# Three gates' state passes in a row, the key-value product behind them, the next tile's keys ahead of the context

## The chip, the cores and the metric

The kernel runs on one core of one Trainium2 chip. The metric is the device time of one execution in microseconds (us); lower is better. The whole input and output stay in fp32.

## What is computed

Eight tiles (`T = 8`) of 512 rows of 128 features. A linear attention, a layer norm, a gated recurrence over the eight tiles, and a second layer norm:

```
Q = elu(x @ Wq.T + bq) + 1;  K = elu(x @ Wk.T + bk) + 1;  V = x @ Wv.T + bv
KV = einsum('bnd,bne->bde', K, V);  Z = einsum('bnd,bd->bn', Q, K.sum(axis=1) + 1e-06)
x  = layernorm(x + (einsum('bnd,bde->bne', Q, KV) / Z[..., None]) @ Wo.T + bo)
# recurrence over the leading axis t = 0..7, state c per row and feature
ft = sigmoid(xt @ wf.T + c @ uf.T + bf);  it = sigmoid(xt @ wi.T + c @ ui.T + bi)
gt = tanh(xt @ wc.T + c @ uc.T + bc);     c  = ft * c + it * gt
h  = tanh(x @ wo.T + c_final @ uo.T + bo);  out = layernorm(x + h)
```

## The kernel before

Every engine has a queue written out by hand, and semaphores tie the queues together. A tile goes through stages that are spread over several tiles in flight. The loop `periods()` runs six times; in period `a` the keys and queries of tile `k = a + 1`, the key-value product and context of tile `a`, the residual and layer norm of tile `b = a - 1`, and the recurrence step of tile `t = a - 2` are worked on. Behind the loop an outro, written call by call, finishes tiles 6 and 7 and steps 4 to 11 (from step 4 on a step handles half a tile, 256 columns), then comes the output projection with the second layer norm.

What each stage does, and its line in the rows:

- `keys` (PE, L430): eight matmuls into the one bank `ps_k`. `key_exp` (ACT, L771), `key_max` (DVE, L1048) turn them into `k_rows`; `key_bias` (ACT, L841) then puts the bias into `ps_k` for the next `keys`. `keys(n)` waits for all three of the tile before.
- `queries` (PE, L448 to L454), `query_exp` (ACT), `query_sum` (DVE, L1106). `x_high` and `x_low` (DVE, L1100) split the next tile's columns into two parts.
- `keys_x` (PE, L463), copied by `xk_copy` (ACT, L855); `key_sums` on POOL (L330, L335). From both `key_values` on PE (L473, L474) makes the key-value product, and `key_values` on DVE (L1114) writes it to `kvo`.
- `context` (PE, L483) waits for `kvo`. `reciprocal_z` (DVE, L1027), `residual` (L1036), `statistics` (L1006), `variance` (L1012), the root on POOL (L339) and `normalise` (DVE, L1021) make the first layer norm.
- `x1_turned` (PE, L497) transposes the normed tile into the one bank `ps_x1`; `x1_high` (ACT, L859) and `x1_low` (DVE, L1043) split it; `x1_whole` (ACT, L863) copies it and frees the bank.
- `gates_x` (PE, L517, L519, L526): nine passes, six that need the high part of the tile and then three that need the low part. `gate_s` (PE, L544, L546, L549): three passes of one gate with the old state, `gates_s` all three gates. Then the three tanh (ACT, L785), `kept_state` (DVE, L1059), `new_state` (L1066), `next_state` (L1073), `state_high` (ACT, L801), `state_low` (POOL, L371).

The order of PE in periods 3 to 5 before is: `keys(k)`, a transpose in period 3, `queries(k)`, `gates_x(t)`, `keys_x(a)`, the forget gate's state passes, `key_values(a)`, the other two gates' state passes, `context(a)`, `x1_turned(b)`. The order of DVE from `attention_end(b)` on is: residual, statistics, variance, `key_max(k)`, `query_sum(k)`, `x_low(k + 1)`, `key_values(a)`, `normalise(b)`, `kept_state(t)`, `new_state(t)`, `reciprocal_z(a)`, `next_state(t)`, `x1_low(b)`.

Of the kernel before, what the change touches and what calls it, by code (L numbers as in the profile page):

```python
# [86 lines left out]
def build(nc, x, xt, w_kq, w_vo_in, w_gate, w_out, rows, att_row, out):  # L87
    with ExitStack() as ctx:
# [323 lines left out]
        def _(pe):  # L412
# [118 lines left out]
            def gates_x(k):  # L531
                for g in range(GATES):
                    gate_x_high(g, k)
                for g in range(GATES):
                    gate_x_low(g, k)
# [131 lines left out]
            for k, a, b, t in periods():  # L667
                if a == 0:

                    keys_x(a)  # L670
                    keys(k)
                    key_values(a)
                    queries(k)
                    context(a)
                    continue

                keys(k)
                if a == 1:
                    keys_x(a)
                if a in (2, 3):  # L680
                    x1_turned(a - 2)
                queries(k)
                if t == 0:

                    gate_x_high(0, t)
                    keys_x(a)
                    gate_x_low(0, t)
                    gate_x_high(1, t)
                    key_values(a)
                    gate_x_low(1, t)  # L690
                    gate_x_high(2, t)
                    gate_x_low(2, t)
                    context(a)
                    continue
                if t is not None:
                    gates_x(t)
                    keys_x(a)
                    gate_s(0, t)
                key_values(a)
                if a == 1:  # L700
                    setup_gates()
                if t is not None:
                    gate_s(1, t)
                    gate_s(2, t)
                context(a)
                if b >= 2:
                    x1_turned(b)

            keys(7)
            queries(7)  # L710
            gates_x(4)
            keys_x(6)
            gate_s(0, 4)
            key_values(6)
            keys_x(7)
            gate_s(1, 4)
            gate_s(2, 4)
            context(6)
            key_values(7)
            x1_turned(5)  # L720
            context(7)
            gates_x(5)
            gates_s(5)
            gates_x(6)
            gates_s(6)
            x1_turned(6)
            out_x(0)
# [33 lines left out]
        def _(act):  # L761
# [112 lines left out]
            for k, a, b, t in periods():  # L874
                if a == 0:
                    xk_copy(a)
                key_exp(k)
                if a == 1:
                    xk_copy(a)
                    act.wait_ge(halved_ok, 1)  # L880
                    nc.scalar.activation(wgate_hi[:, GATES:2 * GATES], wgate[:, GATES:2 * GATES],
                                         ACT.Copy).then_inc(split_hi, 1)
                if t is not None and t >= 1:
                    state_high(t - 1)
                if t is not None:
                    x1_whole(t)
                if a == 2:
                    xk_copy(a)
                query_exp(k)
                if b == 0:  # L890
                    first_normalise(b)
                if a == 0:

                    act.wait_ge(gate_in, 16)
                    nc.scalar.activation(wgate_hi[:, 0:GATES], wgate[:, 0:GATES], ACT.Copy).then_inc(split_hi, 1)
                if k + 1 >= FIRST_SPLIT:
                    x_high(k + 1)
                if a > 2:
                    xk_copy(a)
                if t is not None:  # L900
                    forget_tanh(t)
                    key_bias(k + 1)
                    input_tanh(t)
                if b is not None:
                    x1_high(b)

            key_exp(7)
            state_high(3)
            x1_whole(4)
            query_exp(7)  # L910
            xk_copy(6)
            forget_tanh(4)
            xk_copy(7)
# [44 lines left out]
        def _(dve):  # L958
# [128 lines left out]
            def attention_end(b):  # L1087

                residual(b, range(H, C), y_small_ok)
                residual(b, range(H), y_ok)  # L1090
                dve.wait_ge(y_ok, b + 1)
                dve.wait_ge(y_small_ok, b + 1)
                statistics(b)
                variance(b)
# [28 lines left out]
            for k, a, b, t in periods():  # L1123
# [23 lines left out]
                    query_sum(k)  # L1147
                if k + 1 >= FIRST_SPLIT:
                    x_low(k + 1)
                if a > 2:  # L1150
                    key_values(a)
                normalise(b)
                if a == 1:
                    split_low()
                    first_biases()
                    query_sum(k)
                if t is not None:
                    kept_state(t)
                    new_state(t)
                    reciprocal_z(a)  # L1160
                    next_state(t)
                if b >= 1:
                    x1_low(b)

            attention_end(5)
            key_max(7)
            query_sum(7)
            key_values(6)
            normalise(5)
            kept_state(4)  # L1170
            new_state(4)
            reciprocal_z(6)
            key_values(7)
            next_state(4)
            residual(6, range(H, C), y_small_ok)
            x1_low(5)
            residual(6, range(H), y_ok)
# [129 lines left out]
```

## Time and profile before

| | |
|---|---|
| three runs | 100.78, 101.58 and 101.7 us, median 101.58 us |
| the profiled execution | 101.45 us, of which the span from first to last instruction is 99.7 us |
| PE, DVE, ACT, POOL busy | 90.2, 83.8, 68.8 and 39.9 us |
| granted TensorE clock, mean | 0.975; it is down only in the last two of 40 slices |

PE is TensorE's matmuls, DVE is VectorE, ACT is ScalarE, POOL is GpSimd. The 1.75 us between the execution's time and its span lie ahead of the first and behind the last instruction. In the rows below, matmuls overlap: the next one starts before the one ahead of it has ended, so what a group takes is read from start to start.

### The profile page before, as it was taken

Reading aid. Unit: us, or ns where it says so; the run is one execution under the profiler, and the core shown is the slowest. Engines: PE = TensorE matmul, PEld = TensorE weight load, DVE = VectorE, ACT = ScalarE, POOL = GpSimd, SP = SyncE. Lnnn points to the kernel's source line nnn. Section 1 sums busy time; section 2 is a strip of 40 time slices with the busy share of each in tenths; the row PEclk is TensorE's granted clock in tenths of the full one; section 3 lists DMA queues with packets and bytes.
Section 4 is the critical chain, followed back from the end, with each engine's and each line's share of the span. In section 5 each row is a group of like instructions: output and inputs, shape, how many; then the busy total and the mean of one; then the engine's idle time right before and its main releaser. Section 6 shows DMA issues by size and latency. Waiting matters only on the chain.

```text
span 99.7 us, 1926 instructions
## 1 busy us (share of the span) xinstructions
PE 90.2 (91%) x610; PEld 79.0 (79%) x610; DVE 83.8 (84%) x240; ACT 68.8 (69%) x143; POOL 39.9 (40%) x55
## 2 busy tenths in 40 slices
PE   5998999999999999999999999999999999999000
PEld 4677798778687888898899899999999999896000
DVE  3058489997999999999999989999857897999970
ACT  1428479479698588869778546759586678899460
POOL 3006198508447317606903812440110324445750
PEclk9999999999999999999999999999999999999955
DMA  1868999100000000000000000000000002032636
GB/s 33 290 227 316 396 398 360 54 0 3 0 0 0 0 7 0 3 0 0 0 0 0 0 7 0 0 7 0 7 0 0 0 0 101 5 112 92 224 105 211
DMA packets 5413, 7.36 MB, mean 74 GB/s; under 512 B 507, under 2 KB 3228, under 8 KB 5404
## 3 DMA queue, kind: packets, MB, share of 16 engines
q1 hardware_dynamic: 4972, 6.92, 19.3%
q10 hardware_dynamic: 432, 0.33, 1.3%
q8 instruction: 5, 0.08, 0.3%
q14 instruction: 4, 0.03, 0.1%
HBM read 5.15 MB, written 2.10 MB: 73 GB/s over the span
## 4 chain that ended last, share of the span: by engine, by line
PE 72%; DVE 14%; ACT 6%; issue 2%; POOL 1%; DVEq 0%; ACTq 0%
PE ps_k L430 8%; PE ps_ctx L483 7%; PE ps_ctx L463 6%; DVE stats L1218 4%; PE ps_x L497 4%; PE ps_f L417 4%; DVE x L1237 4%; PE ps_q L454 3%; DVE x L1207 2%; PE ps_ctx L473 2%; PE ps_f L517 2%; PE ps_ctx L474 2%; PE ps_f L526 1%; ACT k_exp L771 1%; PE ps_c L517 1%
## 5 line engine op out<-in xcount | busy, mean ns | idle before, releaser
L371 POOL TENSOR_TENSOR s_lo<-s,s_hi 128x512 fp32r<-128x512 f32 (+1 forms) x6 | 6.7, 1110 | 23.1 <-ACT s_hi L801 23.1
L339 POOL TENSOR_TENSOR rstd<-var_eps,minus_half 128x4 f32<-128x4 f32 x8 | 8.7, 1090 | 8.1 <-DVE var_eps L1012 7.9
L364 POOL TENSOR_TENSOR rstd<-var_eps,minus_half 128x4 f32<-128x4 f32 (+1 forms) x9 | 8.8, 983 | 3.5 <-DVE var_eps L1225 3.3
L330 POOL TENSOR_TENSOR k_pair<-k_rows 128x256 f32<-128x256 f32 x8 | 6.2, 780 | 9.5 <-DVE k_rows L1048 9.5
L859 ACT ACTIVATE x_hi<-ps_x 128x512 fp32r<-128x512 f32 x8 | 4.8, 603 | 6.6 <-PE ps_x L497 6.6
L1021 DVE TENSOR_SCALAR x<-x,stats,rstd 128x128 f32<-128x128 f32 x28 | 9.3, 390 | 0.0
L430 PE MATMUL ps_k<-wkq,x_cols 128*128 128x128 f32 x64 | 9.2, 290 | 0.0
L771 ACT ACTIVATE k_exp<-ps_k,minus_one 128x512 f32<-128x512 f32 x8 | 5.5, 687 | 5.3 <-PE ps_k L438 4.4
L430 PEld LDWEIGHTS ps_k<-wkq,x_cols 128*128 128x128 f32 x64 | 8.4, 204 | 0.7 <-DMA wkq<-w_kq 0.6
L1036 DVE SCALAR_TENSOR_TENSOR x<-ps_ctx,z_inv,x_rows 128x128 f32<-128x128 f32 x28 | 8.0, 342 | 0.1
L483 PEld LDWEIGHTS ps_ctx<-kvo,q_cols 128*128 128x128 f32 x56 | 7.1, 191 | 1.1 <-issue 0.9
L463 PEld LDWEIGHTS ps_ctx<-k_rows,x_rows 128*128 128x128 f32 x56 | 7.1, 191 | 1.0 <-issue 0.7
L463 PE MATMUL ps_ctx<-k_rows,x_rows 128*128 128x128 f32 x56 | 7.5, 277 | 0.4 <-DVE k_rows L1048 0.4
L483 PE MATMUL ps_ctx<-kvo,q_cols 128*128 128x129 f32 x56 | 7.5, 277 | 0.0
L1066 DVE SCALAR_TENSOR_TENSOR new<-th_i,th_c 128x256 f32<-128x256 f32 (+1 forms) x12 | 6.1, 509 | 1.5 <-ACT th_c L785 1.4
L1073 DVE SCALAR_TENSOR_TENSOR s<-keep,new 128x256 f32<-128x256 f32 (+1 forms) x12 | 6.2, 513 | 0.8
L1006 DVE BATCH_NORM_STATS2 stats<-x 128x6 f32<-128x256 f32 x16 | 6.2, 426 | 0.2
L827 ACT ACTIVATE x<-x,shift,rstd 128x128 f32<-128x128 f32 x13 | 5.6, 485 | 1.0 <-DVE shift L1231 0.8
L1048 DVE SCALAR_TENSOR_TENSOR k_rows<-k_exp,ps_k 128x512 f32<-128x512 f32 x8 | 5.4, 681 | 1.0 <-ACT k_exp L771 1.0
L776 ACT ACTIVATE q_exp<-ps_q,wkq 128x512 f32<-128x512 f32 x8 | 5.5, 687 | 0.9 <-PE ps_q L454 0.8
L1059 DVE SCALAR_TENSOR_TENSOR keep<-th_f,s 128x256 f32<-128x256 f32 (+1 forms) x11 | 5.4, 490 | 0.8 <-ACT th_f L785 0.8
L801 ACT ACTIVATE s_hi<-s 128x256 fp32r<-128x256 f32 (+1 forms) x10 | 4.9, 497 | 1.7 <-DVE s L1073 1.6
(219 smaller groups left out, 292.1 us busy)
## 6 DMA issues: line engine op xcount, KB each, us to landing
x_cols<-xt SPq DMA_DIRECT2D x8, 256.0 KB, 7.0
x_rows<-x SPq DMA_DIRECT2D x8, 256.0 KB, 7.0
out<-x SPq DMA_DIRECT2D x7, 256.0 KB, 2.2
wgate<-w_gate SPq DMA_DIRECT2D x1, 384.0 KB, 6.5
out<-x SPq DMA_DIRECT2D x2, 128.0 KB, 2.0
wkq<-w_kq ACTq DMA_DIRECT2D x1, 131.0 KB, 4.0
wvo_in<-w_vo_in ACTq DMA_DIRECT2D x1, 128.0 KB, 4.0
wout<-w_out SPq DMA_DIRECT2D x1, 128.0 KB, 6.7
```

The costliest lines, as they stand in the source:

```text
L330: nc.gpsimd.tensor_tensor(k_pair[:], k_rows[:, a % 2, 0:C // 2], k_rows[:, a % 2, C // 2:C], ALU.add).then_inc(k_pair_ok, 1)
L339: nc.gpsimd.tensor_tensor(rstd[:, b], var_eps[:, b], minus_half[:], ALU.pow).then_inc(rstd_ok, 1)
L364: nc.gpsimd.tensor_tensor(part_of(rstd, u, T), part_of(var_eps, u, T), minus_half[:, 0:nt * H].rearrange("p (t c) -> p t c", c=H), ALU.pow ...
L371: nc.gpsimd.tensor_tensor(s_lo[:, t % 2, part], state(t)[:, part], s_hi[:, t % 2, part].bitcast(F32), ALU.subtract).then_inc(slo_ok[k], 1)
L430: mm = nc.tensor.matmul(ps_k[:, c * D:(c + 1) * D], x_cols[:, a, c], wkq[:, WK_T * D:(WK_T + 1) * D], start=(c == 0 and a < BIAS_BY_PE), s ...
L463: mm = nc.tensor.matmul(small(a)[:, 0:D], x_rows[:, a, c], k_rows[:, a % 2, c], start=(c == 0), stop=(c == C - 1))
L483: mm = nc.tensor.matmul(ctx_of(b, c // 2)[:, c % 2], q_cols[:, b % 2, c], kvo[:, b % 2], start=True, stop=True, skip_group_check=True)
L771: nc.scalar.activation(k_exp[:, a % 2].rearrange("p c d -> p (c d)"), ps_k[:], ACT.Exp, bias=minus_one[:, 0:1]).then_inc(k_exp_ok, 1)
L1006: st = nc.vector.bn_stats(stats[:, b, c:c + 2].rearrange("p c m -> p (c m)"), x1[:, b, c:c + 2].rearrange("p c d -> p d c"))
L1021: nc.vector.tensor_scalar(x1[:, b, c], x1[:, b, c], mean_of(b, c), rstd[:, b, c:c + 1], ALU.subtract, ALU.mult).then_inc(x1_ok, 1)
L1036: ins = nc.vector.scalar_tensor_tensor(x1[:, b, c], ctx_of(b, c // 2)[:, c % 2, 0:D], z_inv[:, b % 2, c:c + 1], x_rows[:, b, c, 0:D], ALU. ...
L1073: nc.vector.scalar_tensor_tensor(state(t)[:, part], keep[:, part], 0.5, new[:, part], ALU.mult, ALU.add).then_inc(s_ok, 1)
```

## The change

On PE, `keys(k)` leaves the head of periods 4 and 5 and of the outro; `keys(k + 1)` is put between `key_values(a)` and `context(a)` of periods 3 to 5. The three gates' state passes of steps 1 to 4 stand in a row ahead of `key_values(a)`. In step 6 the third gate's first passes are put last. On ACT, `key_exp` follows `keys` to the end of the period, ahead of `x1_high`, and `x1_whole` goes behind `query_exp` in periods 4 and 5 and in the outro. On DVE, `key_values(a)` moves from ahead of `normalise(b)` to behind `kept_state(t)`, `next_state(t)` ahead of `reciprocal_z(a)`, and `x1_low` of tiles 2 to 4 into the following `attention_end`, behind the residual. No instruction is added or taken away.

```diff
@@ PE
-                keys(k)
+                if a <= 3:
+                    keys(k)
...
                 if t is not None:
                     gates_x(t)
                     keys_x(a)
-                    gate_s(0, t)
+                    gates_s(t)
                 key_values(a)
...
                 if t is not None:
-                    gate_s(1, t)
-                    gate_s(2, t)
+                    keys(k + 1)
                 context(a)
...
-            keys(7)
             queries(7)
             gates_x(4)
             keys_x(6)
-            gate_s(0, 4)
+            gates_s(4)
             key_values(6)
             keys_x(7)
-            gate_s(1, 4)
-            gate_s(2, 4)
             context(6)
...
             gates_s(5)
-            gates_x(6)
+            for g in (0, 1):
+                gate_x_high(g, 6)
+            for g in (0, 1):
+                gate_x_low(g, 6)
+            gate_x_high(2, 6)
+            gate_x_low(2, 6)
             gates_s(6)
@@ ACT
-                key_exp(k)
+                if a <= 3:
+                    key_exp(k)
...
-                if t is not None:
+                if a in (2, 3):
                     x1_whole(t)
                 if a == 2:
                     xk_copy(a)
                 query_exp(k)
+                if a > 3:
+                    x1_whole(t)
...
                     forget_tanh(t)
                     key_bias(k + 1)
                     input_tanh(t)
+                if t is not None and t >= 1:
+                    key_exp(k + 1)
                 if b is not None:
                     x1_high(b)
 
-            key_exp(7)
             state_high(3)
+            query_exp(7)
             x1_whole(4)
-            query_exp(7)
@@ DVE, attention_end(b)
                 residual(b, range(H, C), y_small_ok)
                 residual(b, range(H), y_ok)
+                if b >= 3:
+                    x1_low(b - 1)
@@ DVE, the loop
-                if a > 2:
-                    key_values(a)
                 normalise(b)
...
-                if t is not None:
+                if t == 0:
                     kept_state(t)
                     new_state(t)
                     reciprocal_z(a)
                     next_state(t)
-                if b >= 1:
+                if t is not None and t >= 1:
+                    kept_state(t)
+                    key_values(a)
+                    new_state(t)
+                    next_state(t)
+                    reciprocal_z(a)
+                if b == 1:
                     x1_low(b)
...
-            key_values(6)
             normalise(5)
             kept_state(4)
+            key_values(6)
             new_state(4)
+            next_state(4)
             reciprocal_z(6)
             key_values(7)
-            next_state(4)
             residual(6, range(H, C), y_small_ok)
```

## Rows read from the trace of the kernel before

**Rows 1.** The page's fourth part: the chain that ended last, by engine.
```profile
PE 72%; DVE 14%; ACT 6%; issue 2%; POOL 1%; DVEq 0%; ACTq 0%
```

**Rows 2.** Busy time of each engine in two stretches, one period of PE each.
```profile
core 0: us, PE busy (x) PEld busy (x) DVE busy (x) ACT busy (x) POOL busy (x), PEclk, DMA share, GB/s
34.80:43.25 8.45, 8.45 (x56) 7.44 (x55) 8.37 (x21) 6.77 (x12) 3.81 (x4) 1.00 0.01 3
43.25:51.69 8.44, 8.44 (x55) 7.44 (x55) 8.36 (x21) 6.76 (x12) 3.82 (x4) 1.00 0.00 0
```

**Rows 3.** Timeline of PE, a period in full flow: start, us, instruction, output and inputs.
```profile
41.76 1.05 PE L483 MATMUL ps_ctx<-kvo,q_cols 128*128 128x129 f32 x8
42.65 0.60 PE L497 MATMUL ps_x<-ident,x 128*128 128x128 f32 x4
43.09 1.06 PE L430 MATMUL ps_k<-wkq,x_cols 128*128 128x128 f32 x8
43.90 0.48 PE L448 MATMUL ps_q<-x_hi,wq_hi 128*128 128x512 f32 x1
...
44.68 0.39 PE L517 MATMUL ps_f<-x_hi,wgate_hi 128*128 128x512 f32 x1
...
46.77 1.05 PE L463 MATMUL ps_ctx<-k_rows,x_rows 128*128 128x128 f32 x8
...
48.36 0.39 PE L473 MATMUL ps_ctx<-bias_z,k_sum 128*128 128x129 f32 x2
```

**Rows 4.** Timeline of PE in period 3, the first with state passes.
```profile
30.29 0.48 PE L544 MATMUL ps_f<-s_hi,wgate_hi 128*128 128x512 f32 x1
...
33.24 1.13 PE L483 MATMUL ps_ctx<-kvo,q_cols 128*128 128x129 f32 x8
...
35.45 0.47 PE L448 MATMUL ps_q<-x_hi,wq_hi 128*128 128x512 f32 x1
```

**Rows 5.** Timeline of DVE in period 3.
```profile
31.68 1.25 DVE L1100 TENSOR_TENSOR x_lo<-x_cols,x_hi 128x512 fp32r<-128x512 f32 x1
32.86 0.28 DVE L1114 TENSOR_TENSOR kvo<-ps_ctx,eps_z 128x129 f32<-128x129 f32 x1
33.06 1.10 DVE L1021 TENSOR_SCALAR x<-x,stats,rstd 128x128 f32<-128x128 f32 x4
34.08 0.68 DVE L1059 SCALAR_TENSOR_TENSOR keep<-th_f,s 128x512 f32<-128x512 f32 x1
```

**Rows 6.** Timeline of ACT, the transposed tile's high part; in brackets idle time and releaser.
```profile
43.29 0.60 ACT L859 ACTIVATE x_hi<-ps_x 128x512 fp32r<-128x512 f32 x1 [0.64 <-PE ps_x L497]
```

**Rows 7.** Timeline of DVE at the end of period 5 and in the outro.
```profile
52.59 0.68 DVE L1043 TENSOR_TENSOR x_lo<-ps_x,x_hi 128x512 fp32r<-128x512 f32 x1
53.19 1.12 DVE L1036 SCALAR_TENSOR_TENSOR x<-ps_ctx,z_inv,x_rows 128x128 f32<-128x128 f32 x4
...
55.82 0.68 DVE L1106 SCALAR_TENSOR_TENSOR q_cols<-q_exp,q_relu 128x512 f32<-128x512 f32 x1
...
56.71 1.53 DVE L1021 TENSOR_SCALAR x<-x,stats,rstd 128x128 f32<-128x128 f32 x4
58.16 0.41 DVE L1059 SCALAR_TENSOR_TENSOR keep<-th_f,s 128x256 f32<-128x256 f32 x1
```

**Rows 8.** Timeline of POOL in the outro.
```profile
55.39 1.02 POOL L339 TENSOR_TENSOR rstd<-var_eps,minus_half 128x4 f32<-128x4 f32 x1 [0.21 <-DVE var_eps L1012]
56.38 0.72 POOL L330 TENSOR_TENSOR k_pair<-k_rows 128x256 f32<-128x256 f32 x1
```

**Rows 9.** Timeline of PE in the outro.
```profile
53.11 0.28 PE L517 MATMUL ps_f<-x_hi,wgate_hi 128*128 128x256 f32 x1
...
54.18 1.06 PE L463 MATMUL ps_ctx<-k_rows,x_rows 128*128 128x128 f32 x8
...
55.78 0.46 PE L473 MATMUL ps_ctx<-bias_z,k_sum 128*128 128x129 f32 x2 [0.16 <-ACT xk L855]
...
57.92 1.05 PE L483 MATMUL ps_ctx<-kvo,q_cols 128*128 128x129 f32 x8
```

**Rows 10.** The list of waits: who waited for whom, us in total, times, longest.
```profile
PEld ps_k L517 <- DVE x L1036: 0.2, 1, 0.2
```

## The prediction, made before the changed kernel was run

> **What bounds the kernel now.** I read the page's chain first: 72% of it lies on PE, 14% on DVE, and none of the waits in it is long [rows 1]. Then the busy time by stretches: in the two full periods PE is busy for all of 8.45 and 8.44 us, and DVE for 8.37 and 8.36 [rows 2]. So in the steady part PE has no gap that a new order could close, DVE is only just behind it, and the same work in another order can't make a period shorter. Gaps that could be closed are the few in period 3 and the outro: 0.16 us at `key_values(6)` [rows 9] and 0.2 us at step 6's third gate, which waits for the residual of tile 7 [rows 10]. On the other side every gap that the new order opens is paid in full, since from period 3 to the outro's end PE never gets ahead of its work.
>
> What PE needs, from start to start: the context's eight matmuls 42.65 - 41.76 = 0.89, the transposes 0.44, keys 0.81, queries 0.78, nine gate passes 46.77 - 44.68 = 2.09, so 0.23 each [rows 3]. From `key_values` at 48.36 to the next context at 50.20 (41.76 and 8.44) lie six passes, 1.40, which leaves 0.44 for the product. Keys ahead of the context are taken at the context's 0.89.
>
> **Period 3, `kvo(3)`.** Before, `key_values(3)` on DVE runs at 32.86, ahead of the normalise, and the context starts at 33.24, 0.10 after its end [rows 4, 5]. Up to there DVE's queue is as before and without a gap, so its next instruction still starts at 32.86. Now come the normalise (34.08 - 33.06 = 1.02) and `kept_state` (0.68, less the 0.08 by which neighbours overlap) ahead of it: `kvo(3)` starts at 34.49, ends at 34.77, and the context can start at 34.87. PE is there earlier: state passes from 30.29 [rows 4], nine of them 2.18 (the first one after an fp32 group takes 0.32), product 0.44, `keys(5)` 0.89, so at 33.80. It waits 1.07 us. Context and refill take 0.96 as before (35.45 less keys, less transposes, less 33.24), transposes without keys behind them 0.36, so `queries(5)` start at 36.19 against 35.45 [rows 4]: **+0.74**. What was gained is in this sum: no wait for the product's inputs, and the keys are already done. The moved keys add a wait of their own, for `key_bias`, which stands behind the forget gate's tanh in ACT's queue: two instructions of 0.6 to 0.7 us like that of rows 6, while PE has six passes and the product, 1.84, to do; nothing is lost. They hide 0.89 of the DVE work; without them the wait would be 1.96. Behind the waiting context nothing on PE can pass, and DVE's `reciprocal_z` waits for it.
>
> **Three times the transposed tile.** `x1_high` on ACT starts 43.29 - 42.65 = 0.64 after the transposes' start and ends at 1.24 [rows 3, 6]. The gates' first pass needs it. Before, keys and queries lay between: 44.68 - 42.65 = 2.03 [rows 3]. With the keys gone it is 2.03 - 0.89 = 1.14, less than 1.24 and the 0.10 of a signal. PE waits 0.20 and needs 0.07 to refill (0.96 against 0.89 at the context): 0.27 in periods 4 and 5 and in the outro, together **+0.8**. Bounds: nothing, if the first pass starts early by the overlap that the timeline draws, and 0.4 each, if `key_exp`, now ahead of `x1_high` in ACT's queue, is late; `keys` end one context (0.89) before the transposes start, and its 0.69 fits into that, so I take 0.27. `state_high` on ACT and `state_low` on POOL now follow `x1_high`; they are needed only behind `gates_x` and `keys_x`, 2.9 us of PE's work later [rows 3].
>
> **`x1_low` behind the residual.** It costs 0.60 wherever it stands [rows 7]. After the context's end come reciprocal 0.17, residual 1.15, `x1_low` 0.68, so it ends some 2.2 after the transposes' start. The low passes of a full step come after six high ones, at about 2.8: nothing in periods 4 and 5. In the outro the six are half as wide, (54.18 - 53.11) / 9 = 0.12 each [rows 9], and come at 2.1: 0.2 lost, but the next point takes its place.
>
> **DVE's chain to `kvo(6)`.** `queries(7)` now start at 52.34 (8.44 after 43.90, rows 3) + 0.74 + 2 x 0.27 = 53.62, the transposes at S = 53.26. From S: the context's end and reciprocal to 0.38, residual to `query_sum` 55.82 - 53.19 = 2.63 and `x1_low` 0.60, to 3.61; `query_sum` 0.60, to 4.2; the root of 1.02 ends about there too [rows 8]; normalise 58.16 - 56.71 = 1.45 [rows 7], `kept_state` 0.34, `kvo` 0.29 and the signal: 6.48. So `context(6)` starts at 59.74 against 57.92 [rows 9]. PE itself, with two `keys_x`, `gates_x`, the state passes and the product, would be there at S + 6.0, so it waits about 0.5. The shift is now 1.8. Step 6's new order gives back the 0.2 of its wait and a refill [rows 10]: **+1.6** when PE goes on. From there to the last 20 us nothing changes in the order, PE is full, and the tail on DVE starts from a gate of PE; the shift is carried to the end. `next_state` ahead of the reciprocal puts 0.6 between `kvo` and it, while the context takes 0.89: nothing. Of the other moves, `x1_whole` behind `query_exp` costs nothing: it only has to be done before the next transposes, seven microseconds later.
>
> **A rule weighed.** The normalise of tile 5 takes 1.53 for the same four instructions that take 1.10 in period 3, and POOL's `k_pair` runs at 56.38 to 57.10 beside it [rows 5, 7, 8]; `x_low` takes 1.25 where other 512-wide DVE instructions take 0.68 [rows 5, 7]. That DVE and POOL hold each other up explains both. If the normalise of tile 5 were not held up, `context(6)` would be 0.43 earlier and the sum +1.2. The Trainium skill, "SBUF — State Buffer", section "Who interferes with whom", says that an instruction of DVE with two SBUF inputs, or in a two-port mode, and a GpSimd instruction that reads SBUF exclude each other for their whole length; by that rule, with which these rows agree, the hold-up stays.
>
> **Sum.** The execution of 101.45, + 0.74 + 0.54 + 0.5 (third stall and chain) - 0.2 = 103.05, so 103.1. The runs' median lies 0.13 higher than the profiled execution, which I leave out.
>
> **The rivals.** *Faster: the order closes the gaps and opens none.* The product behind nine passes no longer waits for `xk`: in the outro it starts at 55.78, where `keys_x` at 54.18 with 0.81 and three half passes with 0.44 would allow 55.43, so 0.35 [rows 9]; step 6 no longer waits, 0.2 [rows 10]; and in period 3 the context starts at 33.24 where passes from 30.29 and the product would allow 32.91, so 0.33 [rows 4]. Together 0.9, so 100.55. The point from which it decides: DVE must have `kvo(3)` written by 33.7, but it stands behind a queue without a gap until 34.77. For it speaks only that modelled ends and POOL's spans are rough. Chance 0.09.
> *Swallowed.* Only period 3's +0.74 stays, the transposes' high part comes in time, and what is saved at the outro's product and at step 6 (0.35 and 0.2) sets off the rest: 101.4 to 102.5, likeliest 102. For it: the 0.20 wait rests on a difference of two tenths. Against it: the chain to `kvo(6)` has two tenths less to spare than it needs even so. Chance 0.24.
> *DVE becomes the bound of every period.* Its work is 8.4 of 8.4 [rows 2]. From the context's end to the next `kvo` now lie residual, `x1_low`, statistics, keys, queries, `x_low`, normalise and `kept_state`, some 7.0, and the context itself is 0.89 to 1.1: 8.1 to 8.2, below PE's 8.7 with its waits. Were each normalise held up as that of tile 5, 0.43 more, it would be 8.6; still no more than PE. With another half microsecond per period 104. Chance 0.07.
>
> **How the numbers follow.** My forecast has 0.60. Its own range: without the refills and with a free normalise + 0.8 less 0.25, 102.0; with 0.4 at each transpose and nothing back at step 6, 103.9. Less than 1% is no more than a measurement of this kernel can tell from no change, here 100.6 to 102.6 around the median. The forecast's lower end falls into that with 0.05. Faster by over 1% has 0.09 less what is too small, 0.07; within 1% 0.24 + 0.05 + 0.02 = 0.31; slower 0.62. The range of 8 in 10 takes in the upper half of the swallowed case: 101.6 to 103.9.
>
> **What would show it.** Right: in period 3 an idle PE of about 1 us ahead of the context, released by DVE's L1114; in periods 4 and 5 a first gate pass that waits for ACT's `x_hi`; 8.7 us per period; `context(6)` released by `kvo`; no wait at step 6's third gate. Wrong: DVE running ahead of PE in period 3, a period of 8.44 still, or a tail on DVE that starts no later than now.

## The result, and the profile after

The changed kernel takes 103.81 us (median of 6 runs, 103.16 to 104.03) against 101.47 us (6 runs, 100.74 to 101.83) on the same chip: a ratio of 1.0236, 95% interval 1.0201 to 1.0272. Its profiled execution took 103.16 us, its span is 101.4 us; 101.45 and 99.7 us before.

The chain that ended last, by engine, has moved from PE to DVE and to waiting ("issue") [rows 1]:

```profile
PE 69%; DVE 17%; issue 5%; ACT 5%; POOL 1%; DVEq 0%; ACTq 0%
```

Busy time of each engine in the two full periods, from one `queries` to the next, with the columns of [rows 2]:

```profile
35.57:44.35 8.78, 8.70 (x56) 7.43 (x55) 8.29 (x20) 6.61 (x12) 3.81 (x4) 1.00 0.01 3
44.35:53.13 8.78, 8.70 (x56) 7.44 (x55) 8.39 (x21) 6.61 (x12) 3.81 (x4) 1.00 0.00 0
```

A period is 8.78 us against 8.44 before. The work is the same; what was added is a wait.

PE in period 3 and at the head of period 4 (to be read against [rows 4] and [rows 3]):

```profile
32.16 1.06 PE L430 MATMUL ps_k<-wkq,x_cols 128*128 128x128 f32 x8
34.25 1.13 PE L483 MATMUL ps_ctx<-kvo,q_cols 128*128 128x129 f32 x8 [1.03 <-issue]
35.22 0.60 PE L497 MATMUL ps_x<-ident,x 128*128 128x128 f32 x4
35.57 0.47 PE L448 MATMUL ps_q<-x_hi,wq_hi 128*128 128x512 f32 x1
...
36.60 0.47 PE L517 MATMUL ps_f<-x_hi,wgate_hi 128*128 128x512 f32 x1
```

DVE in period 3, against [rows 5]:

```profile
30.92 1.26 DVE L1108 TENSOR_TENSOR x_lo<-x_cols,x_hi 128x512 fp32r<-128x512 f32 x1
32.10 1.24 DVE L1027 TENSOR_SCALAR x<-x,stats,rstd 128x128 f32<-128x128 f32 x4
33.27 0.67 DVE L1065 SCALAR_TENSOR_TENSOR keep<-th_f,s 128x512 f32<-128x512 f32 x1
33.87 0.27 DVE L1122 TENSOR_TENSOR kvo<-ps_ctx,eps_z 128x129 f32<-128x129 f32 x1
```

ACT at two of the three transposes, against [rows 6]:

```profile
35.85 0.60 ACT L861 ACTIVATE x_hi<-ps_x 128x512 fp32r<-128x512 f32 x1 [1.91 <-PE ps_x L497]
...
44.63 0.60 ACT L861 ACTIVATE x_hi<-ps_x 128x512 fp32r<-128x512 f32 x1 [0.64 <-PE ps_x L497]
```

Both waits that were foretold stand in these rows. `kvo(3)` ends at 34.14 and the context starts at 34.25, though `keys(5)` from 32.16 take 0.89 and PE was there at 33.05: 1.20 from start to start. The page puts the wait down to "issue", without a name; that it is `kvo` follows from DVE's row, which ends 0.11 before. And the first gate pass, at 36.60, starts 0.15 after `x_hi` ends at 36.45; the three query passes before it need 0.78 and would have let it start at 36.35.

The outro: DVE against [rows 7], POOL against [rows 8], PE against [rows 9].

```profile
51.81 0.69 DVE L1072 SCALAR_TENSOR_TENSOR new<-th_i,th_c 128x512 f32<-128x512 f32 x1 [0.22 <-ACT th_c L787]
...
54.47 0.68 DVE L1049 TENSOR_TENSOR x_lo<-ps_x,x_hi 128x512 fp32r<-128x512 f32 x1
...
57.17 1.80 DVE L1027 TENSOR_SCALAR x<-x,stats,rstd 128x128 f32<-128x128 f32 x4
58.89 0.41 DVE L1065 SCALAR_TENSOR_TENSOR keep<-th_f,s 128x256 f32<-128x256 f32 x1
59.22 0.28 DVE L1122 TENSOR_TENSOR kvo<-ps_ctx,eps_z 128x129 f32<-128x129 f32 x1
```

```profile
57.11 0.73 POOL L330 TENSOR_TENSOR k_pair<-k_rows 128x256 f32<-128x256 f32 x1
```

```profile
54.16 0.36 PE L517 MATMUL ps_f<-x_hi,wgate_hi 128*128 128x256 f32 x1
...
55.21 0.38 PE L526 MATMUL ps_f<-x_lo,wgate_hi 128*128 128x256 f32 x1
...
57.62 0.38 PE L473 MATMUL ps_ctx<-bias_z,k_sum 128*128 128x129 f32 x2
...
59.61 1.13 PE L483 MATMUL ps_ctx<-kvo,q_cols 128*128 128x129 f32 x8 [0.49 <-issue]
...
65.48 0.32 PE L517 MATMUL ps_k<-x_hi,wgate_hi 128*128 128x256 f32 x1
```

`context(6)` is released by `kvo` (59.50), the product no longer waits for `xk`, and step 6's third gate starts without a wait.

**How the kernels are compared below.** The head of the span varies from execution to execution: before, the first weights of `keys(0)` wait 0.64 us for the load of `wkq`, and in the changed kernel's profile they don't. The transposes of period 3, `x1_turned(1)`, start at 25.64 before, at 24.88 after, and between 24.81 and 26.16 in the other kernels, none of which is altered ahead of them. So I count from that instruction. Before, `context(6)` starts 57.92 - 25.64 = 32.28 later and the span ends 74.06 later; after, 34.73 and 76.52. The change costs **2.45 us by `context(6)` and 2.46 at the end**. The medians say 2.34. Each ratio is to the kernel before on the same chip, whose median was 101.24 beside e1 to e4, 101.30 beside e5 to e8 and 101.45 beside e9 to e12. Most rows rest on 4 runs, e11 on 10, e6, e7 and e12 on 12; a fourth run of e4, in a slow state at 181.44 us, is left out. Line numbers of DVE and ACT differ by a few from kernel to kernel; the names of the tiles don't.

| kernel | median us | ratio to before, 95% interval | `x1_turned(1)` | `context(6)` | span | shift at `context(6)` | at the end |
|---|---|---|---|---|---|---|---|
| after | 103.81 | 1.024, 1.020 to 1.027 | 24.88 | 59.61 | 101.4 | +2.45 | +2.46 |
| e1_kvo3_early | 103.23 | 1.020, 1.014 to 1.026 | 25.65 | 60.20 | 102.0 | +2.27 | +2.29 |
| e2_keys_back | 106.61 | 1.053, 1.047 to 1.060 | 25.20 | 62.30 | 104.1 | +4.82 | +4.84 |
| e8_keys_back_high_first | 104.75 | 1.038, 1.031 to 1.045 | 25.16 | 60.80 | 102.5 | +3.36 | +3.28 |
| e3_turned_first | 102.79 | 1.014, 1.009 to 1.019 | 24.93 | 59.23 | 101.0 | +2.02 | +2.01 |
| e4_pool_later | 102.80 | 1.014, 1.006 to 1.021 | 25.88 | 59.22 | 101.4 | +1.06 | +1.46 |
| e5_turned_pool | 102.59 | 1.014, 1.008 to 1.019 | 25.57 | 58.94 | 101.1 | +1.09 | +1.47 |
| e9_row_only | 103.21 | 1.016, 1.011 to 1.022 | 24.86 | 58.56 | 100.5 | +1.42 | +1.58 |
| e10_low_later | 102.83 | 1.015, 1.010 to 1.019 | 24.92 | 59.29 | 101.0 | +2.09 | +2.02 |
| e11_keys_only | 102.20 | 1.009, 1.006 to 1.012 | 26.16 | 59.35 | 101.1 | +0.91 | +0.88 |
| e6_before_pool | 101.21 | 0.998, 0.995 to 1.001 | 24.81 | 56.95 | 98.7 | -0.14 | -0.17 |
| e7_before_step6 | 101.27 | 1.000, 0.996 to 1.003 | 25.36 | 57.63 | 99.3 | -0.01 | -0.12 |
| e12_before_pool_step6 | 100.89 | 0.996, 0.993 to 1.000 | 25.35 | 57.42 | 99.1 | -0.21 | -0.31 |

### The profile page after: what moved, and what is told of

Read it like the earlier page. It is cut to its first block, busy times and chain, and to the rows that moved or that the text cites. A ratio compares the mean times of both kernels' runs of the same rounds, so it can differ in the third digit from the quotient of the medians.

```text
span 101.4 us, 1926 instructions
## 1 busy us (share of the span) xinstructions
PE 90.2 (89%) x610; PEld 79.0 (78%) x610; DVE 84.7 (84%) x240; ACT 68.2 (67%) x143; POOL 39.8 (39%) x55
## 4 chain that ended last, share of the span: by engine, by line
PE 69%; DVE 17%; issue 5%; ACT 5%; POOL 1%; DVEq 0%; ACTq 0%
PE ps_ctx L463 7%; PE ps_k L430 6%; PE ps_ctx L483 6%; DVE stats L1230 4%; PE ps_f L417 4%; DVE x L1249 4%; PE ps_q L454 3%; PE ps_x L497 3%; DVE x L1219 2%; PE ps_f L517 2%; PE ps_f L526 2%; DVE new L1072 2%; DVE s L1079 2%; ACT th_i L787 1%; PE ps_i L526 1%
## 5 line engine op out<-in xcount | busy, mean ns | idle before, releaser
L1027 DVE TENSOR_SCALAR x<-x,stats,rstd 128x128 f32<-128x128 f32 x28 | 10.1, 416 | 0.0
L430 PE MATMUL ps_k<-wkq,x_cols 128*128 128x128 f32 x64 | 8.6, 277 | 0.0
```

Of the source, the lines that this page charges most:

```text
L430: mm = nc.tensor.matmul(ps_k[:, c * D:(c + 1) * D], x_cols[:, a, c], wkq[:, WK_T * D:(WK_T + 1) * D], start=(c == 0 and a < BIAS_BY_PE), s ...
L1027: nc.vector.tensor_scalar(x1[:, b, c], x1[:, b, c], mean_of(b, c), rstd[:, b, c:c + 1], ALU.subtract, ALU.mult).then_inc(x1_ok, 1)
```

## Experiments on the changed kernel

**e1_kvo3_early: is it `kvo(3)` behind `kept_state` that costs period 3?** In period 3 alone `kvo` goes back ahead of the normalise.

```diff
+                if a == 3:
+                    key_values(a)
                 normalise(b)
...
                     kept_state(t)
-                    key_values(a)
+                    if a > 3:
+                        key_values(a)
```

> The changed kernel, but DVE writes kvo(3) ahead of the normalise of tile 2, as before the change; kvo(4) to kvo(6) stay behind kept_state. Theory A (DVE's queue is the bound wherever a new wait shows): PE's 1.03 us ahead of context(3) go, but normalise, kept_state, new_state, next_state and the reciprocal are as late as they were, so x1_low(2) ends at about the same time and PE waits some 0.6 us ahead of the low gate passes of period 4; of 1.1 us only about 0.5 come back: 103.3 us. Rival B (the wait at context(3) is a cost of its own, placed by the order of two instructions): all of 1.0 to 1.1 us comes back, 102.7 us.

The wait at `context(3)` is gone, but the end moves by 0.17 us only. The timeline of PE has the reason:

```profile
33.83 1.06 PE L483 MATMUL ps_ctx<-kvo,q_cols 128*128 128x129 f32 x8
...
38.36 0.50 PE L526 MATMUL ps_f<-x_lo,wgate_hi 128*128 128x512 f32 x1 [0.62 <-DVE x_lo L1049]
```

`queries(5)` come 0.38 earlier than before the change (9.43 against 9.81 after `x1_turned(1)`), then the low passes stop PE for 0.62. DVE's rows name a single wait there, 0.17 ahead of `kvo`, and its `x_lo` is ready no earlier than in the changed kernel (12.65 against 12.51 after `x1_turned(1)`), so PE meets DVE at the next tile that it needs. The 103.3 of the one theory is met, not the 102.7 of the other. The wait for `kvo(3)` is not a cost of its own: it is one of the places where PE is brought back to DVE's pace.

**e3_turned_first: do the transposes ahead of the context take the `x_hi` wait away?**

```diff
                     keys(k + 1)
-                context(a)
                 if b >= 1:
                     x1_turned(b)
+                context(a)
```

> The changed kernel, but in periods 3 to 5 the transposes of tile b stand ahead of the context of tile a. They fill 0.44 us of the wait ahead of context(3), and x_hi is ready when the gates ask for it. Theory A: PE then waits for DVE instead: ahead of the low passes of steps 2 and 4 and still ahead of context(6), and only 0.2 to 0.3 us come back, 103.5 us. Rival C: 0.44 + 3 x 0.33 = 1.4 us come back, 102.4 us.

Periods are 8.69 and 8.66 (`queries` at 35.20, 43.89, 52.55) in place of 8.78, and the first gate passes wait for nothing. But half of the wait for `kvo(3)` remains, and the low passes of the outro now wait:

```profile
34.31 1.13 PE L483 MATMUL ps_ctx<-kvo,q_cols 128*128 128x129 f32 x8 [0.52 <-issue]
...
54.83 0.38 PE L526 MATMUL ps_f<-x_lo,wgate_hi 128*128 128x256 f32 x1 [0.62 <-DVE x_lo L1049]
```

The end gains 0.45 us, and the time lies between the two that were expected. A period is still 0.22 to 0.25 longer than before the change; what takes it is seen in e5.

**e4_pool_later: what does POOL's work beside DVE cost?** POOL's `key_sums(a)`, from tile 4 on, waits until the normalise of tile `a - 2` is done, so the two no longer overlap.

```diff
             def key_sums(a):
+                if a >= 4:
+                    pool.wait_ge(x1_ok, x1_done(a - 2, C - 1))
```

> The changed kernel, but POOL's key sums of tiles 4 to 7 wait until DVE has written the whole normalise of two tiles before, so that they no longer run beside x_low and normalise. If DVE and POOL hold each other up: x_low takes 0.7 instead of 1.24 us, the normalise 1.1 instead of 1.24, and 1.1 instead of 1.8 in the outro; PE's wait ahead of context(3) falls from 1.03 to about 0.2, that ahead of context(6) goes, 1.3 us come back: 102.5 us, all of it by an engine that is not the bound of a period. If the long instructions are long by themselves: durations and time stay, 103.8 us, or a little more by the added wait.

DVE, POOL and PE in the timeline of this kernel:

```profile
31.93 0.68 DVE L1110 TENSOR_TENSOR x_lo<-x_cols,x_hi 128x512 fp32r<-128x512 f32 x1
...
34.36 1.01 DVE L1074 SCALAR_TENSOR_TENSOR new<-th_i,th_c 128x512 f32<-128x512 f32 x1
...
57.44 1.12 DVE L1029 TENSOR_SCALAR x<-x,stats,rstd 128x128 f32<-128x128 f32 x4
...
58.68 0.79 POOL L332 TENSOR_TENSOR k_pair<-k_rows 128x256 f32<-128x256 f32 x1 [1.28 <-PE ps_ctx L476]
...
61.90 0.68 PE L485 MATMUL ps_k<-kvo,q_cols 128*128 128x129 f32 x4 [0.70 <-DVE kvo L1124]
```

`x_low` falls from 1.26 to 0.68, the normalise of the outro from 1.80 to 1.12, `context(6)` waits for nothing and comes 1.39 us earlier than in the changed kernel. Of this 0.4 is given back at once: the late key sums of tile 7 hold `key_values(7)`, and with it the context of tile 7, for 0.70; in period 3 they now lie beside `new`, which takes 1.01 in place of 0.67. The gain at the end is 1.0 us against the 1.3 that the expected 102.5 allowed. By `queries(7)` the shift is 0.83 in place of 1.55, and all of that 0.7 comes from period 3, where the wait at `context(3)` falls from 1.03 to 0.31; periods 4 and 5 stay at 8.76 and 8.78, since there PE waits for `x_hi` and not for DVE. In the old order the same edit for the tiles of the periods gives nothing that can be told (e6, below).

**e5_turned_pool: both edits.** The two diffs above together.

> The changed kernel with both edits: transposes ahead of the context in periods 3 to 5, and POOL's key sums of tiles 4 to 7 behind the normalise. Theory A (PE's losses in the changed kernel are all waits for DVE's chain or for x_hi): ahead of context(3) no more than 0.1 us of wait, periods 4 and 5 at 8.44 to 8.5 us on PE, no wait ahead of context(6), but 0.7 us ahead of context(7), whose key sum now comes late, as in the run with POOL's edit alone: 101.8 us against 101.4 before. If the new order had a cost in itself beyond its waits: 102.5 us.

102.59 us: the rival's number, 102.5, not 101.8. Its reason, a cost beyond the waits, doesn't show: what is left are waits for DVE again, at places that theory A left out. The end is where e4's was (+1.47 and +1.46): the gain of the transposes is taken by the low passes. PE waits 0.37 and 0.62 for them in period 4 and in the outro, and 0.73 for `kvo(7)`. In period 5, DVE and PE:

```profile
44.73 1.13 DVE L1044 SCALAR_TENSOR_TENSOR x<-ps_ctx,z_inv,x_rows 128x128 f32<-128x128 f32 x4
...
45.77 0.68 DVE L1051 TENSOR_TENSOR x_lo<-ps_x,x_hi 128x512 fp32r<-128x512 f32 x1
...
46.51 0.51 PE L528 MATMUL ps_f<-x_lo,wgate_hi 128*128 128x512 f32 x1
46.85 0.39 PE L528 MATMUL ps_i<-x_lo,wgate_hi 128*128 128x512 f32 x1
```

The pass ahead starts at 46.16, so the low pass could at 46.39; it comes at 46.51, behind `x_lo`, and the one after it 0.11 late: 0.23, the whole excess of this period's 8.66 over 8.44. DVE is busy for 7.96 of the 8.66 here, so it isn't a full DVE that makes the period long, but the residual ahead of the low part. No order tried brought the changed kernel back to the one before.

**e2_keys_back: how much do the moved keys hide?** Keys and `key_exp` go back to the head of the period; the row of state passes, `kvo` behind `kept_state` and the late low passes stay.

```diff
-                if a <= 3:
-                    keys(k)
+                keys(k)
...
-                if t is not None:
-                    keys(k + 1)
                 context(a)
...
+            keys(7)
             queries(7)
@@ ACT
-                if a <= 3:
-                    key_exp(k)
+                key_exp(k)
...
-                if t is not None and t >= 1:
-                    key_exp(k + 1)
...
+            key_exp(7)
             state_high(3)
```

> The changed kernel, but keys(5) to keys(7) and their key_exp stand at the head of the period again; gate passes in a row, kvo and x1_low stay. Both theories: the first gate pass of periods 4, 5 and of the outro no longer waits for x_hi (0.33 each), and PE waits about 2.0 instead of 1.03 us ahead of context(3). Theory A: in the outro DVE's chain from context(5) to kvo(6) decides, and context(5) starts 0.4 us earlier than in the changed kernel, so 103.4 us, with the wait ahead of context(6) still there. Rival B, sum of PE's waits: 0.9 more and 1.0 less, 103.7 us. Rival C (the transposes' wait for ACT is the main cost of the change): 102.8 us or less.

Much slower than any of the expectations. Besides the wait of 1.92 in period 3 there are waits ahead of the other contexts, and something on DVE that none foresaw. PE ahead of `context(4)`, then POOL and DVE in period 5:

```profile
44.11 1.13 PE L483 MATMUL ps_ctx<-kvo,q_cols 128*128 128x129 f32 x8 [0.86 <-issue]
...
47.90 1.29 POOL L371 TENSOR_TENSOR s_lo<-s,s_hi 128x512 fp32r<-128x512 f32 x1 [5.54 <-ACT s_hi L801]
47.98 1.24 DVE L1014 TENSOR_SCALAR var_eps<-stats 128x4 f32<-128x4 f32 x1
```

A variance of 128 x 4 values takes 1.24 us where it takes 0.17 elsewhere. It starts 0.08 after POOL's `s_lo` and ends with it (49.22 and 49.19). `key_exp` stands here ahead of `state_high` on ACT, so `s_lo` comes later and meets the variance, in periods 4 and 5 and in the outro.

**e8_keys_back_high_first: the same without that meeting.** Otherwise e2, with `state_high` ahead of `key_exp` on ACT from period 4 on.

```diff
+                if t is not None and t >= 2:
+                    state_high(t - 1)
                 key_exp(k)
...
-                if t is not None and t >= 1:
+                if t == 1:
                     state_high(t - 1)
...
-            key_exp(7)
             state_high(3)
+            key_exp(7)
```

> The run with the keys back at the head, with one more edit: ACT makes the state's high part ahead of key_exp, so POOL's 1.29 us subtraction starts about 0.9 us earlier and lies ahead of DVE's variance instead of on it. If POOL's instruction holds the small variance instruction up: its duration falls from 1.24 to about 0.3 us in periods 4, 5 and the outro, the waits ahead of contexts 4 and 5 go from 0.85 to near nothing, 2.3 us come back: 104.3 us. If the variance is long for another reason: 106.5 us.

The variance is back at 0.25 and less, so POOL's instruction was what held it. The end is 1.56 us earlier than e2's, the median 1.86, where 2.3 was expected: the waits at contexts 4 and 5 fall to 0.43 each and not to nothing. What is left, 0.82 over the changed kernel, is what the keys hide there, less the three waits for `x_hi`, which don't occur here. In the timeline DVE now waits for the product, and PE for DVE:

```profile
43.25 0.29 DVE L1120 TENSOR_TENSOR kvo<-ps_ctx,eps_z 128x129 f32<-128x129 f32 x1 [0.43 <-PE ps_ctx L474]
43.65 1.13 PE L483 MATMUL ps_ctx<-kvo,q_cols 128*128 128x129 f32 x8 [0.43 <-issue]
```

## Experiments on the kernel before

Runs e9, e11, e10 and e7 put one part of the change each into the kernel before; e6 and e12 put e4's edit of POOL there.

**e9_row_only: the row of state passes, with the product behind it.**

```diff
                     keys_x(a)
-                    gate_s(0, t)
+                    gates_s(t)
                 key_values(a)
...
-                if t is not None:
-                    gate_s(1, t)
-                    gate_s(2, t)
                 context(a)
...
-            gate_s(0, 4)
+            gates_s(4)
             key_values(6)
             keys_x(7)
-            gate_s(1, 4)
-            gate_s(2, 4)
             context(6)
```

> The kernel before with one part of the change alone: on TensorE the three gates' state passes of steps 1 to 4 stand in a row ahead of key_values(a). Keys, the order of DVE and that of ACT are as before. Theory A, the hand-over: six passes (1.40 us) no longer lie between the product and the context, so the context waits for DVE's kvo. With the keys put back ahead of the period and the row kept, these waits were 0.43, 0.43 and 0.51 us behind kept_state; here kvo is ahead of the normalise, so about 0.45 us each in periods 3 to 5 and at context(6), less 0.35 us that the product of the outro no longer waits for its inputs: about +1.4 us, 102.8 us against a before of 101.4. Theory B, the row itself costs nothing because the passes are only exchanged with the product: within 0.3 us of before.

Theory A holds in its cause, at 103.21 for 102.8. PE and DVE in period 4:

```profile
41.05 0.39 PE L474 MATMUL ps_ctx<-w_vo,xk 128*128 128x128 f32 x2
41.47 0.29 DVE L1109 TENSOR_TENSOR kvo<-ps_ctx,eps_z 128x129 f32<-128x129 f32 x1 [0.79 <-PE ps_ctx L474]
41.86 1.13 PE L483 MATMUL ps_ctx<-kvo,q_cols 128*128 128x129 f32 x8 [0.43 <-issue]
```

The way from the product over DVE to the context lies open three times, and the periods are 9.12 us. DVE idles 0.79 ahead of `kvo`: here neither engine is full, each waits for the other. Its sizes were off both ways: a period costs 0.68 and not 0.45, and nothing waits at `context(6)`. In the outro the product's wait for `xk` is gone and the shift falls from +1.64 at `queries(7)` to +1.42 at `context(6)`.

**e11_keys_only: the keys ahead of the context, and what goes with them on ACT.** The diff is that of e2 read the other way round, on the kernel before, with `x1_whole` moved as in the change; the gates stay split around the product.

> The kernel before with one part of the change alone: keys(k + 1) ahead of the context in periods 3 to 5, and with it key_exp and x1_whole on ACT. The gates stay split around the product, and kvo stays ahead of the normalise. Theory A: only the waits of the first gate pass for the transposed tile's high part come in, 0.33 us each in periods 4, 5 and the outro: +1.0 us, 102.3 us; the context never waits for kvo, since keys (0.9 us) and six passes lie between. Theory B: without kvo behind kept_state TensorE is not held elsewhere, and the waits close something that DVE needs anyway: within 0.3 us of before.

102.2 us where theory A said 102.3. The periods are 8.77 us like those of the changed kernel, with the same start of the gates' first pass 1.38 after the transposes, and no wait for `kvo`:

```profile
44.18 0.60 PE L497 MATMUL ps_x<-ident,x 128*128 128x128 f32 x4
...
45.56 0.47 PE L517 MATMUL ps_f<-x_hi,wgate_hi 128*128 128x512 f32 x1
```

**e10_low_later: the new order of DVE, but for `kvo`.**

```diff
@@ attention_end(b)
                 residual(b, range(H), y_ok)
+                if b >= 3:
+                    x1_low(b - 1)
@@ the loop
                     new_state(t)
-                    reciprocal_z(a)
+                    if t == 0:
+                        reciprocal_z(a)
                     next_state(t)
-                if b >= 1:
+                    if t >= 1:
+                        reciprocal_z(a)
+                if b == 1:
                     x1_low(b)
```

> The kernel before with one part of the change alone: on DVE, in periods 4 and 5 and the outro, x1_low stands behind the next tile's residual, and next_state ahead of the reciprocal in periods 3 to 5. kvo stays ahead of the normalise. Prediction's step: x1_low ends some 2.2 us after the transposes' start and the low passes come at 2.8 (here later still, because keys and queries lie between, at 2.03 + 1.4 = 3.4 us), so nothing in periods 4 and 5; in the outro at most 0.2 us: 101.4 to 101.6 us. Rival: DVE is as full as TensorE, and the reciprocal that now stands 0.6 us later and the residual behind it put x_low, kvo and with them the context 0.2 to 0.5 us later in each period: 102.3 us.

Slower than both expectations. Periods 4 and 5 are 9.23 and 8.88 us. ACT, PE and DVE of period 4:

```profile
37.35 0.60 ACT L863 ACTIVATE x_cols<-ps_x 128x512 f32<-128x512 f32 x1 [1.10 <-DVE x_lo L1043]
37.37 0.50 PE L526 MATMUL ps_f<-x_lo,wgate_hi 128*128 128x512 f32 x1 [0.27 <-DVE x_lo L1043]
...
39.22 0.69 DVE L1108 SCALAR_TENSOR_TENSOR q_cols<-q_exp,q_relu 128x512 f32<-128x512 f32 x1 [0.43 <-ACT q_relu L777]
...
39.94 0.46 PE L473 MATMUL ps_ctx<-bias_z,k_sum 128*128 128x129 f32 x2
```

The late low part stops two queues. PE waits for it before its low passes: from start to start 0.44, and a refill of 0.11 (the pass behind a wait follows later than passes otherwise do). And ACT's `x1_whole` waits for it 1.10, with `query_exp`, the next tile's split and `xk_copy` queued behind; `xk` ends at 39.80, so the product comes 0.18 late with another 0.07 of refill. Together 0.80, which is the period's 0.79. In the outro the low passes wait 0.60 and the product 0.17. The changed kernel moves `x1_whole` behind `query_exp`, and there the product doesn't wait; whether this is `x1_whole`'s move or the product's later place was not tried.

**e7_before_step6: step 6's order alone.** The change's lines of step 6 put into the kernel before.

> The kernel before, with the smallest part of the change alone: in step 6 the third gate's first passes stand last. The 0.2 us wait for the residual of tile 7 goes, and a refill with it: 0.2 to 0.25 us faster, 101.2 us if before is 101.4. Rival (DVE's own chain in the outro is the bound there and hands the gain back): no difference.

In the trace `x1_turned(6)` comes 0.22 us earlier, the end 0.12, and the median of 12 runs doesn't move. The wait is removed, and 0.10 of the gain is lost again at the low passes of step 7: their first starts 0.06 behind DVE's `x_lo`, and the next follows it 0.24 later in place of 0.12. What is left is too small to be told.

**e6_before_pool: POOL's edit in the kernel before,** for tiles 4 to 6 (`if 4 <= a <= 6`).

> The kernel before, with one edit: POOL's key sums of tiles 4 to 6 behind the normalise. x_low takes 0.68 instead of 1.24 us, so DVE is half a microsecond further ahead in each of periods 3 to 5. Theory A: PE bounds those periods in the kernel before, so nothing comes of it there; only the waits in period 3 and that of step 6 for the residual can shrink: 0 to 0.4 us faster, 101.2 us if before is 101.4. Rival (DVE bounds the kernel before as well, as its 8.36 of 8.44 us suggest): over 1 us faster.

No difference that can be told: 0.998, against 1.0 us of e4. The trace gains 0.24 in period 3 and nothing behind it. Before the change PE is full in the periods and DVE's lost half microseconds lie beside it.

**e12_before_pool_step6: both together.**

> The kernel before with the two edits that were free in it together: POOL's key sums of tiles 4 to 6 wait until the normalise beside them is done, and step 6's third gate starts behind the other gates' low passes. Each alone moved the end by 0.1 to 0.2 us in its trace and the median by nothing that could be told. Theory A: both act on TensorE's wait ahead of step 6 or in cover, together 0 to 0.4 us: 101.0 to 101.4 us. Rival: the held-up normalise of the outro (1.53 us) is what sets context(6) in the kernel before, so 0.4 us and the 0.2 us of step 6 add up: 100.8 us or less.

The best version found, 0.4% faster than before (0.05 to 0.7%), just below the 101.0 of theory A and just above the rival's 100.8, so the time doesn't decide between them. DVE's row of period 3 shows `x_lo` at full speed, and who pays for it:

```profile
31.39 0.69 DVE L1107 TENSOR_TENSOR x_lo<-x_cols,x_hi 128x512 fp32r<-128x512 f32 x1
...
34.61 1.04 DVE L1080 SCALAR_TENSOR_TENSOR s<-keep,new 128x512 f32<-128x512 f32 x1
```

Nor was the rival really tried by this kernel: the key sums of tile 7 aren't delayed, and the normalise of the outro still takes 1.61.

## Why the prediction was right, and where its sizes were off

The sign and the mechanism were right: 103.1 was forecast, 103.81 measured, inside the range but 0.09 from its upper end. The profiled execution, 103.16, agrees with the 103.05 of the sum (its terms as written add up to 103.03) better than the sum deserves; that is luck: the part ahead of `x1_turned(1)` was 0.76 us shorter in it. Counted from there the shift is 2.46 us where the prediction had 1.6. Term by term:

- **Period 3, +0.74: measured +0.88** (`queries(5)` 10.69 after `x1_turned(1)`, 9.81 before). PE was ready at 8.17, forecast 8.16. It waited 1.20 from start to start where 1.07 was forecast: `kvo(3)` came 0.14 later, because the normalise took 1.24 and not 1.10. With `kvo` gone from ahead of it, it started 0.40 before POOL's `k_sum` ended, and not 0.19; in e4, with POOL's work elsewhere, it takes 1.11. The sum took its duration from the old order. That the wait is a cost of its own is what the prediction had wrong here: by e1 all but 0.17 of it comes back as another wait.
- **Three times the transposed tile, 0.27 each: measured 0.34** in each period. The signal from ACT to PE is 0.15, not the 0.10 taken from DVE's. e11 shows this term without the rest: +0.32, +0.33 and, by `context(6)`, +0.47, less 0.21 that period 3 gains there, +0.88 at the end. In the changed kernel the third one is no term of its own: `context(6)` hangs on DVE.
- **`x1_low`: nothing in periods 4 and 5.** So it is in the changed kernel, but only because PE has already waited. With the wait at `context(3)` removed (e1) the low passes wait 0.62; with earlier transposes (e3, e5) too; in e10, alone with the later reciprocal, the late low part goes with 2.0 us. In the outro of the changed kernel, where 0.2 was expected, the first low pass comes at 55.21 in place of 54.94, and this is covered as foretold. The step's reasoning counted from the transposes, as if DVE came to `x1_low` free; it was right for the sum and wrong as a statement on its slack.
- **DVE's chain to `context(6)`: 6.48 forecast, 6.83 measured** from the transposes of the outro (59.61 - 52.78). The normalise is 0.27 of it, 1.80 for 1.53: it starts 0.06 after `k_pair` and not 0.33, so it is held for nearly all of `k_pair`'s 0.73. Another 0.27 is the chain's head, put at 0.38 and measured 0.65: the residual starts at 53.43. By the rows DVE was still busy with `new_state`, which had waited 0.22 for ACT's `th_c` (51.81), and with `next_state`, whose move ahead of the reciprocal the prediction put at nothing. Two slips hid this: residual to `query_sum` took 0.11 less than forecast, and the terms as written add up to 6.39, not 6.48. PE's wait was forecast from start to start as "about 0.5"; by that measure it is 0.74, since `keys_x(7)` from 58.06 take 0.81. That the row prints 0.49 is no agreement.
- **Step 6, -0.2:** the shift falls from 2.53 at the gates of step 5 (62.55) to 2.31 at `x1_turned(6)` (66.94), and 0.15 is lost again by the end. 0.12 of it lies at the low passes of step 7, as in e7: PE gained on the order of step 6, DVE didn't, its `x_lo` ends at 69.05, the first low pass starts at 69.11, and the next follows 0.23 later in place of 0.12. By e7 nothing of the gain reaches the median.
- **`x1_whole` behind `query_exp` costs nothing:** right, no row waits for it in the periods; in e10, where it stays ahead while the low part is late, the product comes 0.18 late and refills for 0.07.
- **A rule weighed.** The hold-up between DVE and POOL stayed, and grew. The prediction carried it as a row of fixed length, and priced its absence at 0.4, for the normalise of the outro alone; e4 gains 1.0.

0.14, twice 0.07, 0.35, 0.08 for the refill of the waiting `context(6)` and 0.15 behind step 6 make 0.86, and 2.46 less 1.6 is 0.86. Five small terms, all too low.

**The rivals.** *Faster* didn't occur: DVE had `kvo(3)` at 34.14, a microsecond after PE wanted it. *Swallowed* didn't either; e9, e10 and e11 show that each part alone is slower, by 1.6, 2.0 and 0.9 us. They sum to 4.5 and together, with `kvo`'s move, cost 2.5, so part of the change works against its other parts. That the keys cover the hand-over which e9 lays open is shown by e8, without them 0.82 slower; that `x1_whole`'s move takes the second half of e10's loss is read from the rows, and the product's later place would explain it as well. *DVE as the bound of every period* isn't what the changed kernel shows, at 8.78 with DVE busy for 8.29 and 8.39; but something of DVE's is near everywhere, since each edit that freed PE (e1, e3, e5) met a wait for one of its results.

Open is what `kvo`'s move behind `kept_state` costs in periods 4 and 5 and in the outro, of which no run was made alone, and what the key sums of tile 7 would give if they were placed free of both the normalise and `key_values(7)`; it wasn't tried.

## What to carry to other kernels

Here two engines were both full over a period; what the new order gave one was paid by the other, and where one wait was removed most of it came back at the next tile handed over. In such a kernel look for what the waiting engine would meet next, not for the longest wait. Work that lies between a product, its copy and its use is not in the way: it is the cover of the hand-over, and whatever replaces it has to be as long as the way over the other engine. Durations of instructions that another engine holds up belong to the order, not to the instruction: take them anew for the place where it will start.

## What the runs showed of the hardware

DVE and POOL stop each other for whole instructions, even when one is tiny: in e2 the variance of 128 x 4 took 1.24 us beside a POOL subtraction of 1.29 that had started 0.08 before, and 0.17 away from it. POOL is held too: in the changed kernel `k_sum` took 0.79 where it started beside DVE's `x_low` (31.71) and 0.46 in the outro. `x_lo<-ps_x,x_hi`, with one input from PSUM, isn't held: in e4 it starts 0.07 behind the same subtraction and takes its 0.68.

```profile
37.41 0.68 DVE L1051 TENSOR_TENSOR x_lo<-ps_x,x_hi 128x512 fp32r<-128x512 f32 x1
37.34 1.31 POOL L373 TENSOR_TENSOR s_lo<-s,s_hi 128x512 fp32r<-128x512 f32 x1 [1.65 <-ACT s_hi L805]
```

The Trainium skill, "SBUF — State Buffer", section "Who interferes with whom", says of DVE's two-port modes that whoever issues first gets the shared ports for the whole instruction and the other blocks fully, and that an instruction of DVE with at most one SBUF input outside the two-port modes isn't affected; the traces agree with both.

A wait of PE costs more than the idle time in its row. In e10 the row says 0.27 at the low passes; from start to start the delay is 0.44, since the matmul ahead is drawn to its modelled end, and the next pass follows 0.34 after in place of 0.23. The whole is 0.55.
